# Expert feed-forward of a gated decoder block: second product by rows, queue rows loaded in two layouts

## The reference, cut to what matters

```python
capacity = 160                                   # floor(1.25 * 2048 / 16)
gate_logits = tokens @ gate_w.T                  # tokens = layernorm(x1), 2048 x 256
combine_weights, sec_mask = _top1_router(gate_logits, capacity)
dispatch = jnp.einsum('sec,sd->ecd', sec_mask, tokens)     # 16 x 160 x 256
h = jax.nn.gelu(jnp.einsum('ecd,edf->ecf', dispatch, w1))  # w1: 16 x 256 x 1024
expert_out = jnp.einsum('ecf,efd->ecd', h, w2)             # w2: 16 x 1024 x 256
out = jnp.einsum('sec,ecd->sd', combine_weights, expert_out)
x = x1 + jnp.tanh(g_ffn[0]) * out
```

## Time and profile before

| what | value |
|---|---|
| median of 3 runs | 350.33 us (349.52 to 351.09) |
| the profiled execution's own time | 352.72 us |
| its span, first to last instruction | 350.6 us |
| mean granted TensorE clock | 0.972 |
| PE busy | 319.6 us (91%) |
| PE weight loads busy | 276.3 us (79%) |
| DVE busy | 187.8 us (54%) |
| ACT busy | 172.8 us (49%) |
| POOL busy | 148.0 us (42%) |
| moved by DMA | 60.70 MB, mean 173 GB/s |

### The profile page before, as it was taken

The page is one execution under the profiler, slowest core; times in us unless marked ns, Lnnn a source line. Parts: engine busy times, 40 slices in busy tenths (PEclk is TensorE's granted clock), DMA queues, the critical chain, the costliest instruction groups (busy, mean ns, idle before and its releaser), DMA issues.

```text
span 350.6 us, 8454 instructions
## 1 busy us (share of the span) xinstructions
PE 319.6 (91%) x2884; PEld 276.3 (79%) x2884; DVE 187.8 (54%) x926; ACT 172.8 (49%) x650; POOL 148.0 (42%) x179
## 2 busy tenths in 40 slices
PE   8868989989999997997979999999999999999980
PEld 4437667877678765776848999999999999999970
DVE  2799788999879895999752221221222222212120
ACT  2489899999969886999212111111111111111110
POOL 6489385578576637656244022222222221112222
PEclk9989999999989999998799999999999999999996
DMA  7900792159511303130053988999989888888200
GB/s 216 314 15 23 240 360 96 27 156 366 183 51 23 93 3 120 25 93 2 0 201 116 288 269 270 287 287 265 280 266 267 274 274 286 252 265 262 82 15 12
DMA packets 39429, 60.70 MB, mean 173 GB/s; under 512 B 3208, under 2 KB 27850, under 8 KB 39392
## 3 DMA queue, kind: packets, MB, share of 16 engines
q1 hardware_dynamic: 36032, 53.45, 49.0%
q0 software_dynamic: 2816, 6.25, 5.2%
q10 hardware_dynamic: 544, 0.52, 0.4%
HBM read 44.77 MB, written 14.19 MB: 168 GB/s over the span
## 4 chain that ended last, share of the span: by engine, by line
PE 58%; DVE 13%; ACT 13%; issue 7%; DMA 3%; POOL 3%; DVEq 0%; POOLq 0%; SPq 0%
PE bank L1569 19%; PE bank L1585 18%; ACT probs L611 9%; PE bank L1267 4%; DVE probs L809 4%; PE bank L1214 3%; PE bank L1225 3%; DVE rows L876 2%; PE bank L1595 2%; PE bank L1286 2%; PE bank L1255 2%; ACT q_par L585 2%; PE bank L1236 1%; DVE probsT L828 1%; PE bank L1322 1%
## 5 line engine op out<-in xcount | busy, mean ns | idle before, releaser
L611 ACT ACTIVATE probs<-probs,low 128x128 f32<-128x128 f32 x256 | 99.2, 403 | 1.9 <-DVE low L809 1.9
L739 ACT ACTIVATE w_raw<-bank 128x480 f32<-128x480 f32 (+1 forms) x48 | 25.2, 526 | 125.6 <-PE bank L1569 123.1
L547 POOL DMA_INDIRECT out_dram<-q_rows,place x32 | 29.1, 910 | 125.9 <-issue 109.3
L466 POOL TENSOR_TENSOR probs<-probs,r_total 128x512 f32<-128x512 f32 x64 | 66.4, 1051 | 34.0 <-DVE r_total L818 33.9
L1569 PE MATMUL bank<-xdT,w 128*128 128x160 f32 x512 | 77.6, 300 | 0.7 <-DVE xdT L1128 0.7
L1585 PE MATMUL bank<-w_raw,w 128*128 128x160 f32 x512 | 72.4, 299 | 0.0
L1569 PEld LDWEIGHTS bank<-xdT,w 128*128 128x128 f32 x512 | 71.2, 190 | 0.9 <-issue 0.9
L1585 PEld LDWEIGHTS bank<-w_raw,w 128*128 128x128 f32 x512 | 70.4, 190 | 0.0
L809 DVE CUSTOM_DVE_ANT_0 probs<-bank,mask_now 128x128 f32<-128x128 f32 x256 | 57.3, 284 | 4.1 <-PE bank L1255 3.6
L611 ACT ACTIVATION_READ_ACCUMULATOR probs<-probs,low 128x1 f32 x256 | 52.0, 203 | 0.0
L1136 DVE COPY yT<-bank 128x320 f32<-128x320 f32 x16 | 7.9, 492 | 73.5 <-PE bank L1585 73.5
(11 more groups left out here) (121 smaller groups left out, 400.2 us busy)
## 6 DMA issues: line engine op xcount, KB each, us to landing
w<-in_L_ffn_w_dram SPq DMA_DIRECT2D x32, 1024.0 KB, 5.5
expert_queue<-empty_row SPq DMA_DIRECT2D x1, 5140.0 KB, 17.8
q_rows<-expert_queue SPq DMA_DIRECT2D x16, 321.2 KB
ctx_rows<-in_ctx_dram SPq DMA_DIRECT2D x4, 512.0 KB, 9.8
out_dram<-rows SPq DMA_DIRECT2D x4, 512.0 KB, 4.6
x_all<-in_x_dram SPq DMA_DIRECT2D x3, 512.0 KB, 6.7
v_shift<-v SPq DMA_DIRECT2D x12, 128.0 KB, 2.2
x_all<-in_x_dram SPq DMA_DIRECT2D x2, 256.0 KB, 3.7
```

Source lines behind the costliest of these rows:

```text
L466: pool.tensor_tensor(probs[:, i % NP_], probs[:, i % NP_], r_total[:, i % NP_].unsqueeze(2).to_broadcast([P, PAIRS, 2 * WINDOW]), ALU.mult ...
L547: pool.indirect_dma_start(out=out_rows, out_offset=bass.IndirectOffsetOnAxis(ap=place[i][:, s:s + 1], axis=0), in_=q_rows[i][:, s, D:2 * D ...
L611: last = act.activation(probs[:, i % NP_, j], probs[:, i % NP_, j], ACT.Exp, scale=-1.0, bias=low[:, i % NP_, j:j + 1], accum_out=total[:, ...
L739: act.activation(hidden[:, ms[0]:ms[-1] + 1, :], ps_hidden[m][:, 0:n].rearrange("p (m c) -> p m c", c=CAP), ACT.Gelu_apprx_tanh).then_inc( ...
```

## The change

The second product is done the other way round. `hidden` becomes the stationary operand and w2 the moving one, so the result comes as rows of slots. Slots 0 to 127 take 8 matmuls of 128 x 128 against 256 columns into `ps_y`. Slots 128 to 159 (REST = 32) take 8 matmuls of 128 x 32 against 256 columns into `ps_rest`, each of its four quarters of 32 partitions summing two of the eight blocks; they stand between block 5 and block 6 of the other eight, and expert 1's first transposes stand behind them in expert 0. DVE adds the four partial sums one after the other to the rest's rows, each with a wait for the one before. `yT`, its copy and the transposes back are gone. The queue rows are loaded in two layouts: the normalised half in `q_rows` (80 partitions x 2 x 256, for the transposes), and the other 258 words in `base` (128 rows, and 32 rows by a second DMA). `place` and both indirect stores follow the second layout.

```diff
+    REST = CAP - P
-        q_rows = [sb(f"q_rows{i}", [SR, 2, ROW]) for i in range(NQ)]
+        q_rows = [sb(f"q_rows{i}", [SR, 2, D]) for i in range(NQ)]
+        base = [sb(f"base{i}", [P, 2, ROW - D]) for i in range(NQ)]
-        yT = sb("yT", [P, KD, CAP])
-        place = [sb(f"place{i}", [SR, 2], U32) for i in range(NQ)]
+        place = [sb(f"place{i}", [P, 2], U32) for i in range(NQ)]
@@ SP
-                sp.dma_start(q_rows[i][:], queue[bass.ts(e, CAP), :].rearrange("(s p) c -> p s c", p=SR)
+                sp.dma_start(q_rows[i][:], queue[bass.ts(e, CAP), 0:D].rearrange("(s p) c -> p s c", p=SR)
                              ).then_inc(rows_in[i], 16)
+            def load_base(e, i):
+                mine = queue[bass.ts(e, CAP), D:ROW]
+                sp.dma_start(base[i][:, 0], mine[0:P]).then_inc(base_in[i], 16)
+                sp.dma_start(base[i][0:REST, 1], mine[P:CAP]).then_inc(base_in[i], 16)
...
-            for e in (0, 2, 3):
+            load_base(0, 0)
+            load_base(1, 1)
+            for e in (2, 3):
                 load_rows(e, e)
+                load_base(e, e)
...
                 load_rows(NQ * turn + i + NQ, i)
+                load_base(NQ * turn + i + NQ, i)
@@ POOL
-                pool.wait_ge(yrows_taken, e + 1)
+                pool.wait_ge(y_taken, e + 1)
                 pool.sem_inc(pool_waited, 1)
-                for s in range(2):
-                    pool.indirect_dma_start(out=out_rows,
-                                            out_offset=bass.IndirectOffsetOnAxis(ap=place[i][:, s:s + 1], axis=0),
-                                            in_=q_rows[i][:, s, D:2 * D], in_offset=None, bounds_check=B * S - 1,
-                                            oob_is_err=False).then_inc(y_out[i], 16)
+                pool.indirect_dma_start(out=out_rows, out_offset=bass.IndirectOffsetOnAxis(ap=place[i][:, 0:1], axis=0),
+                                        in_=base[i][:, 0, 0:D], in_offset=None, bounds_check=B * S - 1,
+                                        oob_is_err=False).then_inc(y_out[i], 16)
+                pool.wait_ge(rest_taken[3], e + 1)
+                pool.sem_inc(pool_waited, 1)
+                pool.indirect_dma_start(out=out_rows,
+                                        out_offset=bass.IndirectOffsetOnAxis(ap=place[i][0:REST, 1:2], axis=0),
+                                        in_=base[i][0:REST, 1, 0:D], in_offset=None, bounds_check=B * S - 1,
+                                        oob_is_err=False).then_inc(y_out[i], 16)
@@ DVE
-            def take_place(i):
-                dve.tensor_copy(place[i][:], q_rows[i][:, :, 2 * D + 1]).then_inc(place_ready, 1)
+            def take_place(turn, i):
+                dve.wait_ge(base_in[i], 32 * turn + 32)
+                dve.tensor_copy(place[i][0:REST, 1:2], base[i][0:REST, 1, D + 1:D + 2])
+                dve.tensor_copy(place[i][:, 0:1], base[i][:, 0, D + 1:D + 2]).then_inc(place_ready, 1)
+            def add_rest(e, i, j):
+                rest = base[i][0:REST, 1]
+                if j > 0:
+                    dve.wait_ge(rest_taken[j - 1], e + 1)
+                dve.scalar_tensor_tensor(rest[:, 0:D], ps_rest[j * REST:(j + 1) * REST, 0:D], rest[:, D:D + 1],
+                                         rest[:, 0:D], ALU.mult, ALU.add).then_inc(rest_taken[j], 1)
+            def take_y(e, i):
+                dve.wait_ge(rest_ready, e + 1)
+                add_rest(e, i, 0)
+                add_rest(e, i, 1)
                 dve.wait_ge(y_ready, e + 1)
-                dve.tensor_copy(yT[:], ...).then_inc(yT_taken, 1)
+                dve.scalar_tensor_tensor(base[i][:, 0, 0:D], ps_y[:, 0:D], base[i][:, 0, D:D + 1], base[i][:, 0, 0:D],
+                                         ALU.mult, ALU.add).then_inc(y_taken, 1)
+                add_rest(e, i, 2)
+                add_rest(e, i, 3)
@@ PE
-                for d in range(KD):
-                    if first and d == 1:
-                        xdT_of(0, 1)
-                    for k in range(KF):
-                        if d == 0 and k in (0, 3, 6):
-                            pe.wait_ge(gelu_done, 3 * e + k // 3 + 1)
-                        last = pe.matmul(ps_y[:, d * CAP:(d + 1) * CAP], w2_sb[i % 2][:, k, d * P:(d + 1) * P],
-                                         hidden[:, k], start=(k == 0), stop=(k == KF - 1))
+                for k in range(KF):
+                    if k in (0, 3, 6):
+                        pe.wait_ge(gelu_done, 3 * e + k // 3 + 1)
+                    if k == 6:
+                        rest_product(e, i, first)
+                        if first:
+                            xdT_of(0, 1)
+                    last = pe.matmul(ps_y[:, 0:D], hidden[:, k, 0:P], w2_sb[i % 2][:, k], start=(k == 0), stop=(k == KF - 1))
                 last.then_inc(y_ready, 1)
-            def yrows_of(e, first):
...
+            def rest_product(e, i, first):
+                if not first:
+                    pe.wait_ge(rest_taken[3], e)
+                for step in range(KF // 4):
+                    for j in range(4):
+                        k = KF // 4 * j + step
+                        last = pe.matmul(ps_rest[j * REST:(j + 1) * REST, 0:D], hidden[:, k, P:CAP], w2_sb[i % 2][:, k],
+                                         start=(step == 0), stop=(step == KF // 4 - 1))
+                last.then_inc(rest_ready, 1)
```

More of the change, by code:

```diff
@@ L60, in flamingo_kernel @@
     NQ = 4
-    assert (T, KD, NW, HG, UNITS) == (4, 2, 8, 8, 16) and CAP % 32 == 0 and E % NQ == 0 and E > 2 * NQ
+    assert (T, KD, NW, HG, UNITS) == (4, 2, 8, 8, 16) and REST == 32 and E % NQ == 0 and E > 2 * NQ
     out_rows = out.rearrange("b s d -> (b s) d")
@@ L184, in flamingo_kernel @@
         rows_in = [sem(f"rows_in{i}") for i in range(NQ)]
+        base_in = [sem(f"base_in{i}") for i in range(NQ)]
         y_out = [sem(f"y_out{i}") for i in range(NQ)]
@@ L219, in flamingo_kernel @@
         hidden_ready, gelu_done = sem("hidden_ready"), sem("gelu_done")
-        y_ready, yT_taken = sem("y_ready"), sem("yT_taken")
-        yrows_ready, yrows_taken = sem("yrows_ready"), sem("yrows_taken")
+        rest_ready, y_ready = sem("rest_ready"), sem("y_ready")
+        y_taken, rest_taken = sem("y_taken"), [sem(f"rest_taken{j}") for j in range(4)]
         def value(n, per, k):
@@ L340, in _ @@
             sp.wait_ge(scattered[1], 16 * T)
-            sp.dma_start(q_rows[0][:, :, 0:D], queue[0:CAP, 0:D].rearrange("(s p) c -> p s c", p=SR)
+            sp.dma_start(q_rows[0][:], queue[0:CAP, 0:D].rearrange("(s p) c -> p s c", p=SR)
                          ).then_inc(rows_in[0], 16)
@@ L1129, in take_xd @@
                                 ).then_inc(xdT_taken, 1)
-            def take_place(i):
-                dve.tensor_copy(place[i][:], q_rows[i][:, :, 2 * D + 1]).then_inc(place_ready, 1)
-            def take_yT(e):
-                dve.wait_ge(y_ready, e + 1)
[L1136 to L1145, removed]
+            def take_place(turn, i):
+                dve.wait_ge(base_in[i], 32 * turn + 32)
+                dve.tensor_copy(place[i][0:REST, 1:2], base[i][0:REST, 1, D + 1:D + 2])
+                dve.tensor_copy(place[i][:, 0:1], base[i][:, 0, D + 1:D + 2]).then_inc(place_ready, 1)
@@ L1147, in expert @@
             def expert(turn, i, early, late):
                 e = NQ * turn + i
-                if not early or i > 0:
-                    take_yrows(e - 1, (i - 1) % NQ)
                 if not late or i < NQ - 1:
                     take_xd(e + 1, (i + 1) % NQ, early and i == 0)
[L1153 to L1158, removed]
+                take_place(turn, i)
@@ L1160, in _ @@
+                take_y(e, i)
             take_xd(0, 0, True)
@@ L1546, in xdT_of @@
                 e = NQ * turn + i
-                pe.wait_ge(rows_in[i], 16 * turn + (32 if i == 0 else 16))
+                pe.wait_ge(rows_in[i], 16 * turn + 16)
                 pe.wait_ge(xdT_taken, e)
@@ L1576, in second_product @@
                 if not first:
-                    pe.wait_ge(yT_taken, e)
-                for d in range(KD):
-                    if first and d == 1:
-                        xdT_of(0, 1)
-                    for k in range(KF):
-                        if d == 0 and k in (0, 3, 6):
-                            pe.wait_ge(gelu_done, 3 * e + k // 3 + 1)
-                        last = pe.matmul(ps_y[:, d * CAP:(d + 1) * CAP], w2_sb[i % 2][:, k, d * P:(d + 1) * P],
-                                         hidden[:, k], start=(k == 0), stop=(k == KF - 1))
+                    pe.wait_ge(y_taken, e)
+                for k in range(KF):
[6 more added lines that the diff above has]
+                    last = pe.matmul(ps_y[:, 0:D], hidden[:, k, 0:P], w2_sb[i % 2][:, k], start=(k == 0), stop=(k == KF - 1))
                 last.then_inc(y_ready, 1)
-            def yrows_of(e, first):
-                pe.wait_ge(yT_taken, e + 1)
+            def rest_product(e, i, first):
```

(4 more changed lines are left out.)

4 lines of the change are left out of this document (1 added, 3 removed).

## The result

The changed kernel takes 345.38 us in the median of 4 runs (344.49 to 346.13), the kernel before beside it 350.47: a ratio of 0.9866 with a 95% interval of 0.9837 to 0.9895. That is 5.1 us less by the medians, and 3.7 to 5.7 by the interval. The forecast was 345.9, 4.4 less. Medians and ranges count every execution, while the ratios leave out those that ran slow, among them two of 652.74 and 657.79 us in the later sets, whose cause is not known.

What follows compares the result with a forecast made beforehand. PE's own work was taken as the bound: -2.6 us for experts 1 to 15, -0.4 for expert 0 and -1.4 for the tail make -4.4, from the 350.33 median to 345.9 us. The range was 343.5 to 352.0.

Steps and rivals of the forecast that it cites:

- The 128 slots: Second product on PE: 16 records of 256 moving columns at 0.216 us each, 3.45 us added per expert.
- The 32 slots: Burst of 16 records in four quarters on PE, running together as in attend: 1.01 us added per expert, exit included.
- The upper end, 3.45: Burst for slots 128 to 159 if the four quarters did not run together: 16 x 0.216 = 3.45 us.
- An expert: PE's work per expert: -4.79 + 3.45 + 1.01 + 0.16 = -0.17 us, from 9.46 to 9.3.
- Entry: Gap on PE ahead of the 32-slot burst: 0.16 us per expert, the middle between attend's 0.09 and 0.24.
- Expert 0: From its second product to expert 1's start: the wait for expert 1's rows goes, -0.4 us.
- The tail: From the last second product to the last indirect store's issue: 5.1 us becomes 3.7, -1.4 us.
- Sum: Whole kernel: -2.6 for experts 1 to 15, -0.4 for expert 0, -1.4 for the tail, together -4.4 us.
- The low end of -5.9: Whole kernel: largest gain the forecast allowed by its own terms, whose bounds were -5.9 to -2.7 us (344.4 to 347.6).
- What was costed at nothing: DVE's adds, POOL's issues, SP's three loads per expert and DMA traffic: all expected to stay hidden, at no cost.
- the bounds given: DMA's work per expert: 6.8 us at the 381 GB/s of a saturated stretch, 8.5 us by its 0.90 share.
- The rival in which DMA becomes the bound: Expert stage: two more small loads raise the queue's work above 9.3 us per expert; at 10 us, 351 us; 4%.

Runs made afterwards that it cites:

- each edit of PE's work: Changed kernel with the rest's burst done twice, 360.69 us; rest summed into two quarters, 361.12; into one quarter, 388.43; rest left out, 326.92.
- the repeats: The changed kernel run again unedited, twice, beside the kernel before: 346.23 us (ratio 0.983) and 347.1 us (ratio 0.9866).
- the short second product: Changed kernel without matmuls and adds for slots 128 to 159, and with only three of eight feature blocks in the second product: 320.25 us, one run.

## Why the prediction was right

- **What bounds the kernel.** PE's own work did, before and after. Apart from the 0.68 us at the start of the stage, and expert 0's wait for rows before, it waited for nothing; each edit of PE's work came out in the stage one to one (0.86, 0.85, 2.57 and -1.20 us per expert, times 16, against +13.8, +13.6, +41.0 and -19.2 us).
- **The 128 slots.** 3.45 us for 16 records, from one row of a projection: measured 3.45 where they stand together.
- **The 32 slots.** 1.01 us from attend's burst, by counting columns: measured 1.00. The upper end, 3.45, was measured as 3.57 with its exit.
- **An expert.** The turned product costs 0.30 us more than the old one (3.45 + 1.00 + 0.09 + 0.11 against 4.35), and the transposes back give 0.44. So the turn pays only by what it makes needless.
- **Entry.** 0.16 between 0.09 and 0.24 was taken, and 0.09 came. But the wide records behind the burst take 0.11 more, a term that the sum did not have. The two errors cancel in part, which is luck: -0.17 us per expert was forecast, -0.14 came (9.46 to 9.32), or -2.0 for 15 experts in place of -2.6.
- **Expert 0.** -0.4 forecast and -0.4 measured (5.32 to 4.92).
- **The tail.** -1.4 forecast, -1.6 measured (5.10 to 3.51): the big add came 0.04 us behind the last matmul, not 0.2. The two rest adds took 0.98 together, as expected, but the last four records cover more of them: they run for 1.13 us, where the sum had 0.84. The shapes' own rows, three steps and one duration, give 1.03, and the slower restart adds the rest.
- **Behind the last issue.** The sum had nothing here, and -0.2 came: 5.76 us to the end of the span before, where 80 rows are stored last, and 5.53 after, where 32 are.
- **Sum.** -4.4 forecast; -2.0 - 0.4 - 1.6 - 0.2 measured, which is the stage's -4.2. The forecast's experts were 0.6 too good and its tail 0.4 too poor, so the closeness of the sum is partly luck.
- **Slips in the sum's bounds.** With entries of 0.09 and 0.24 an expert is -0.24 to -0.09, not -0.25 to -0.10, and 15 of them -3.6 to -1.4. The low end of -5.9 does not follow from the terms, which give -3.6 - 0.4 - 1.4 = -5.4. The measured time lies inside either way.
- **What was costed at nothing.** DVE, SP and the split loads were all hidden behind PE. DMA's floor is 8.1 us per expert, inside the bounds given. The rival in which DMA becomes the bound needed 9.3.
- **The median.** 5.1 us where the stage has 4.2. The forecast took its 4.4 off the median of before and not off the profiled execution, which stood 2.4 above that median. That was right: the two profiled executions are 8.2 us apart (352.72 and 344.49), of which 3.7 lie ahead of the stage. Of the 5.1, 0.3 stand outside the span and 0.6 are within what the repeats scatter.

What is open: the 0.3 us outside the span, a small gain or loss ahead of the stage, and how much of expert 0's gain is the earlier landing and how much the later need.

## What to carry to other kernels

Count an fp32 matmul by its moving columns, from a row of the same kernel, and ask how many of the four quarters of the output's partitions it fills. Turning this product round cost 0.30 us per expert by itself and paid only by the transposes that it made needless; its odd 32 rows were cheap only because four independent sums could be found for them. Then count the change of shape too, a third of a microsecond here for each burst, and put bursts behind one another. Before cutting PE's work further, measure what DMA needs with PE's work taken away; here there was 1.2 us per expert and no more. And compare two profiles stage by stage from a fixed instruction on, since executions of one kernel reached this stage up to 3.1 us apart.

## What the runs showed of the hardware

- Records of 32 columns of weights whose outputs lie in four different quarters of the partitions run together fully, at 256 moving columns: a second burst of 16 took 0.86 us, against 3.45 (16 steps of 0.216) in one quarter. The records start in fours, 0.22 us apart on average.
- Going into a burst of 32-column weights and out again costs 0.34 us: 0.09 ahead, 0.14 at its end, 0.11 in the records after it. The weight loads show the idle side of it: they stand still for 0.33 us ahead of the burst and 0.41 behind it.

```profile
275.84 0.59 PEld L1613 LDWEIGHTS bank<-w,w_raw 128*32 128x32 f32 x16 [0.33 <-issue]
...
276.84 0.73 PEld L1603 LDWEIGHTS bank<-w,w_raw 128*128 128x128 f32 x4 [0.41 <-issue]
```

- When DMA is saturated, SP's issue of a load is held up: in the short second product one issue of `q_rows` takes 4.28 us, where such issues take 0.35 to 0.94 in the changed kernel.

```profile
240.74 4.28 SPq L300 DMA_DIRECT2D q_rows<-expert_queue  x1
```

- A mix of weights, rows and indirect stores saturates DMA at 322 GB/s, where a stretch of loads and a plain store had 381.
- The end of the span comes 5.53 us behind the end of the last indirect issue when that stores 32 rows (5.53 or 5.54 in all nine profiles of such kernels), 5.75 or 5.76 with 80 rows (two), and 5.87 with 128 rows (one).
